# One signal of TensorE per expert tile, down products two tiles behind, and unpaused late scatters

## What is computed

```python
x = x + layernorm(attn(layernorm(x)))    # x: (8, 512, 128) f32, 16 heads of 8, relu MLP 128-512-128 inside
x = x + layernorm(moe(layernorm(x)))
# moe, for each of the 4096 tokens: softmax router over 8 experts, the best 2 are taken
#   g = x @ gate_w[e].T ; u = x @ up_w[e].T       (128 -> 352)
#   y = (silu(g) * u) @ down_w[e].T               (352 -> 128), summed with the two router weights
```

## Time and profile before

| what | value |
|---|---|
| median of 3 runs | 591.68 us (590.68 to 592.72) |
| span of the profiled execution | 596.4 us |
| TensorE busy | 532.1 us, 89% |
| VectorE, ScalarE, GpSimd busy | 63%, 66%, 59% |
| gate and up products, L871 | 111.5 us in 852 passes |
| down products, L881 | 62.5 us in 426 passes |
| indirect DMAs of GpSimd, L1782 and L1793 | 64 and 71, 143.3 us |

### The profile page before, as it was taken

How to read it: one execution, slowest core, us unless ns; L and a number is a source line. 1 busy time by engine, 2 the same in 40 slices (tenths; PEclk the granted TensorE clock), 3 DMA queues, 4 the chain that set the end, 5 groups by cost and what they waited for, 6 DMA issues and landing times.

```text
span 596.4 us, 14609 instructions
## 1 busy us (share of the span) xinstructions
PE 532.1 (89%) x4952; PEld 395.0 (66%) x4969; DVE 375.9 (63%) x1095; ACT 395.4 (66%) x880; POOL 349.7 (59%) x449
## 2 busy tenths in 40 slices
PE   6989899899899899988899899999976899999981
PEld 5655455556566455655555666889976899999960
DVE  6824583965975947996847877527742365555347
ACT  3388989888978788869788696644531355555425
POOL 6104636545538885357877258487578555565545
PEclk9999999999999999999999999999996799999997
DMA  7245333213213322232734512212122203321174
GB/s 196 76 126 161 111 99 109 74 37 108 80 45 122 102 86 71 77 100 78 201 109 134 132 56 52 59 55 69 55 61 69 55 32 86 88 63 32 33 287 141
DMA packets 47016, 55.62 MB, mean 93 GB/s; under 512 B 7376, under 2 KB 41056, under 8 KB 44784
## 3 DMA queue, kind: packets, MB, share of 16 engines
q1 hardware_dynamic: 42624, 45.76, 26.7%
q0 software_dynamic: 4320, 8.92, 4.5%
HBM read 36.27 MB, written 18.92 MB: 93 GB/s over the span
## 4 chain that ended last, share of the span: by engine, by line
PE 56%; DVE 15%; ACT 10%; POOL 6%; issue 6%; DMA 3%; another core or an unknown queue 3%; DVEq 1%; SPq 0%; ACTq 0%; POOLq 0%
PE SC L871 11%; PE OA L748 9%; PE OA L881 6%; PE M L786 4%; PE M L822 4%; PE SC L730 3%; ACT arena L1015 3%; PE SC L734 2%; PE M L643 2%; DVE SS L1330 2%; PE SC L740 2%; PE M L662 1%; POOL slots L1782 1%; PE M L852 1%
## 5 line engine op out<-in xcount | busy, mean ns | idle before, releaser
L1015 ACT ACTIVATE arena<-SC 128x1024 f32<-128x1024 f32 x160 | 161.9, 1039 | 14.7 <-PE SC L735 11.8
L871 PE MATMUL SC<-arena 128*128 128x128 f32 (+1 forms) x852 | 111.5, 283 | 0.0
L871 PEld LDWEIGHTS SC<-arena 128*128 128x128 f32 (+1 forms) x852 | 104.0, 191 | 0.4 <-issue 0.3
L748 PE MATMUL OA<-arena 128*32 128x256 f32 (+1 forms) x1536 | 88.9, 349 | 6.6 <-DVE arena L455 2.8
L1782 POOL DMA_INDIRECT slots<-XBA,IDX x64 | 72.6, 1134 | 37.0 <-DVE IDX L1455 19.6
L1503 DVE TENSOR_TENSOR arena<-arena,SC 128x256 f32<-128x256 f32 (+1 forms) x142 | 43.7, 348 | 68.6 <-issue 24.6
L881 PE MATMUL OA<-arena 128*128 (+1 forms) x426 | 62.5, 284 | 12.9 <-issue 8.1
L748 PEld LDWEIGHTS OA<-arena 128*32 128x32 f32 x1536 | 39.2, 109 | 44.0 <-issue 22.8
L881 PEld LDWEIGHTS OA<-arena 128*128 128x128 f32 (+1 forms) x426 | 55.2, 198 | 15.4 <-issue 15.4
L454 POOL TENSOR_TENSOR arena<-arena 128x512 f32<-128x512 f32 x32 | 42.7, 1335 | 36.2 <-ACT arena L1015 35.6
L447 POOL TENSOR_TENSOR arena<-arena 128x512 f32<-128x512 f32 x23 | 31.2, 1356 | 48.9 <-ACT arena L1015 48.8
(11 more groups left out here) (244 smaller groups left out, 1086.0 us busy)
## 6 DMA issues: line engine op xcount, KB each, us to landing
arena<-parts SPq DMA_DIRECT2D x90, 192.0 KB
parts<-arena SPq DMA_DIRECT2D x16, 384.0 KB
arena<-ytok SPq DMA_DIRECT2D x8, 512.0 KB, 7.3
XGA<-slots SPq DMA_DIRECT2D x39, 65.0 KB
arena<-slots SPq DMA_DIRECT2D x32, 65.0 KB, 1.9
X<-in_L_attn_x SPq DMA_DIRECT2D x4, 512.0 KB, 5.1
out<-X SPq DMA_DIRECT2D x8, 256.0 KB, 2.5
arena<-parts SPq DMA_DIRECT2D x12, 96.0 KB
```

The source lines that it names most:

```text
L748: mm = pe.matmul(OA[32 * j:32 * j + 32, q0:q0 + n], vals[:, t, 32 * h:32 * h + 32], probs(j), start=first, stop=last, skip_group_check=True)
L871: mm = pe.matmul(SC[0:n, r % 2, 512 * m + P * c:512 * m + P * (c + 1)], WSEL[s % 4][:, I * m + i0:I * m + i0 + n], XGT[r % 2], start=True, ...
L1015: act.activation(EB[u], SC[:, n % 2, :], ACT.Exp).then_inc(exp_done, 1)
```

## The change

TensorE gives one signal per tile, `tile_full`, in place of four. `step(s)` is now: gate of tile `s`, transpose of tile `s + 2`, two of the three up products of `s`, the down product of tile `s - 2`, and the last up product of `s`, which signals. ScalarE waits for that one signal and then does its three jobs in the order copy of tile `s + 2`, result of tile `s - 2`, Silu of `s`. TensorE gets waits for the Silu and the product of tile `s - 2` before it writes their banks again (`sg_rdy`, `h_rdy`). From tile 24 on, odd tiles use the two M1 banks for the transpose and for the result. HTB has three buffers. One step more is run at the end (`STILES + 2`).

GpSimd's clearings are gone. The scatters of batch 5 stand one by one at units 2 to 15 of body 8 (`LATE5_AT`), and all 16 of batches 6 and 7 at unit 3 of body 9 (`LATE67_AT`), ahead of that unit's `put`. `put` runs two tiles behind. Batch 7 has a buffer of its own for its rows (XBL, in the space of the exponentials), and its wait for the scatters of batch 5 moves from VectorE to GpSimd.

```diff
-    dict(yroot=6, aroot=9, xroot=13, sc0=3, sc1=4, sc2=4, sc3=5, sc4=5, sc5=6, sc6=7, sc7=8))
+    dict(yroot=6, aroot=9, xroot=13))
+LATE5_AT = (2, 4, 6, 8, 10, 12, 14, 15)
+LATE67_AT = 3
+DOUBLE = 24
...
+        def turned(s):
+            return (M1S[0] if s >= DOUBLE and s % 2 else M0)[:, 0:P]
+        def result(s):
+            return (M1S[1] if s >= DOUBLE and s % 2 else OA)[:, 0:P]
+        def had_bank(s):
+            return s - 1 if s <= DOUBLE else s - 2 if s > DOUBLE + 1 else -1
...
@@ TensorE
+            def xt(s):
+                r, it = s % RING, s // RING
+                pe.wait_ge(xg_in[r], 16 * (it + 1))
+                if had_bank(s) >= 0:
+                    pe.wait_ge(xt_rdy, had_bank(s) + 1)
...
+                return pe.transpose(turned(s), XG[r][:, 0:D], IDN[:, :])
...
+            def down(s):
+                off = weights_offset(pe, s)
+                pe.wait_ge(h_rdy, s + 1)
+                if had_bank(s) >= 0:
+                    pe.wait_ge(ys_rdy, had_bank(s) + 1)
...
-            def step(s, r, it):
-                if s + 1 < STILES:
-                    xt(s + 1, r + 1, 16 * (it + 1 + (r + 1) // RING))
-                if s < STILES:
-                    gu(s, r)
-                if s >= 1:
-                    down(s - 1, r + 1, woff(s - 1))
+            def step(s):
+                if s < STILES:
+                    pe.wait_ge(wsel_rdy, s + 1)
+                    pe.wait_ge(xt_rdy, s + 1)
+                    if s >= 2:
+                        pe.wait_ge(sg_rdy, s - 1)
+                    half(s, 0, range(NIC))
+                    if s + 2 < STILES:
+                        xt(s + 2)
+                    if s >= 2:
+                        pe.wait_ge(h_rdy, s - 1)
+                    mm = half(s, 1, range(NIC - 1))
+                if s >= 2:
+                    mm = down(s - 2)
+                if s < STILES:
+                    mm = half(s, 1, (NIC - 1,))
+                mm.then_inc(tile_full, 1)
...
@@ ScalarE
+            def step(s):
+                act.wait_ge(tile_full, s + 1)
+                if s + 2 < STILES:
+                    evac_x(s + 2)
+                if s >= 2:
+                    evac_y(s - 2)
                 if s < STILES:
-                    silu(s, r)
-                if s >= 1:
-                    evac_y(s - 1, r - 1)
+                    silu(s)
...
@@ VectorE
-            def hidden(s, r):
+            def hidden(s):
                 dve.wait_ge(sg_rdy, s + 1)
-                dve.wait_ge(up_full, s + 1)
...
@@ GpSimd
                 for k in choices:
-                    if b >= NB - 4:
-                        pause()
                     pool.indirect_dma_start(out=slots_d.ap(), ...)
...
             def put(s, r):
-                pause()
                 pool.wait_ge(ys_rdy, s + 1)
...
+                    if b == NB and n in LATE5_AT:
+                        scatter(NB - 3, LATE5_AT.index(n) // 2, (LATE5_AT.index(n) % 2,))
+                    if b == NB + 1 and n == LATE67_AT:
+                        for k in range(2 * T):
+                            scatter(NB - 2 + k // T, k % T)
                     for s in early_tile(b, n):
-                        if s >= 1:
-                            put(s - 1, (s - 1) % RING)
+                        if s >= 2:
+                            put(s - 2, (s - 2) % RING)
```

More of the change, by code:

```diff
@@ L478, in lots_at, with xb @@
             return [i] if 0 <= i < NWT else []
+        def xb(b):
+            return XBL if b == NB - 1 else XB[b % 2]
+        def turned(s):
[4 more added lines that the diff above has]
+            return s - 1 if s <= DOUBLE else s - 2 if s > DOUBLE + 1 else -1
         def early_tile(b, n):
@@ L853, in weights @@
                 mm.then_inc(wt_full, 1)
[L858 to L867, removed]
-                    pe.wait_ge(xt_rdy, s + 1)
[L869 to L873, removed]
@@ L875, in down @@
-            def down(s, r, off):
-                pe.wait_ge(h_rdy, s + 1)
-                if s >= 1:
-                    pe.wait_ge(ys_rdy, s)
-                for c, (i0, n) in enumerate(IC):
-                    mm = pe.matmul(OA[:, 0:P], HTB[r % 2][0:n, P * c:P * (c + 1)],
-                                   WALL[0:n, bass.ds(off + 2 * I + P * c, P)], start=c == 0, stop=c == NIC - 1)
-                mm.then_inc(y_full, 1)
-            def woff(s):
-                return weights_offset(pe, s)
@@ new lines, in half @@
+            def half(s, m, chunks):
+                for c in chunks:
+                    i0, n = IC[c]
+                    mm = pe.matmul(SC[0:n, s % 2, 512 * m + P * c:512 * m + P * (c + 1)], WSEL[s % 4][:, I * m + i0:I * m + i0 + n],
+                                   XGT[s % 2], start=True, stop=True)
+                return mm
+            def down(s):
[3 more added lines that the diff above has]
+                    pe.wait_ge(ys_rdy, had_bank(s) + 1)
+                for c, (i0, n) in enumerate(IC):
+                    mm = pe.matmul(result(s), HTB[s % 3][0:n, P * c:P * (c + 1)],
+                                   WALL[0:n, bass.ds(off + 2 * I + P * c, P)], start=c == 0, stop=c == NIC - 1)
+                return mm
@@ L908, in early @@
                     pe.wait_ge(table_rdy, 2)
[L909 removed]
+                step(s)
             pe.wait_ge(const_rdy, 1)
@@ L995, in _ @@
             pe.wait_ge(table_rdy, 3)
-            for s in range(EARLY, STILES + 1):
-                step(s, s % RING, s // RING)
-            keep_busy(29)
+            for s in range(EARLY, STILES + 2):
+                step(s)
+            keep_busy(29, SC[:, 0, :])
             for b in BY_TENSOR:
@@ L1169, in _ @@
                     if b == NB and n == 0:
-                        evac_x(0, 0)
-                        step(0, 0)
+                        for s in range(2):
+                            act.wait_ge(xt_full, s + 1)
+                            evac_x(s)
+                        step(0)
                     if b == 0 and n in TABLE_AT:
@@ L1217, in _ @@
                         if s > 0:
-                            step(s, s % RING)
-            for s in range(EARLY, STILES + 1):
-                step(s, s % RING)
+                            step(s)
+            for s in range(EARLY, STILES + 2):
+                step(s)
             act.preload_act_table_set("natural_log_exp_and_others")
```

91 lines of the change are left out of this document (47 added, 44 removed).

## The result

The changed kernel took 611.96 us (610.44 to 614.14, 4 runs) beside 592.2 us (590.68 to 595.68, 4 runs) of the kernel before: a ratio of 1.0317, interval 1.0283 to 1.0351. It is 3.2% slower, where the prediction had 1.6% faster.

A forecast was written before the change was run, and what follows sets the result against it. Late TensorE signals beside GpSimd's indirect DMAs were taken to cost 21.0 us; 21.0 - 3.8 - 3.5 - 1.8 - 2.0 - 0.3 = 9.6 us won of 596.4, scaled to 582.2 us; forecast's range 576 to 589, overall 572 to 594.

The forecast's parts named there:

- one signal per DMA is more than enough for one per 2.12 us: Tiles beside GpSimd's DMAs: with a 1.27 us DMA period, one signal a tile suffices; the stretch gives back 21.0 us.
- One TensorE signal gets through per indirect DMA: Bad stretch, tiles 19 to 39: 1.3 us per signal read as matching GpSimd's 1.49 us period, within 15%.
- Rival B: Slower: clearings let signals through, so the unbroken scatter block stops TensorE 18.4 us; 6.8 us slower, 598.4 us; chance 0.16.
- Tile distance: Down product two tiles behind: 0.6 us to spare per tile, taken as 0, bound 6 us.
- Loads: Tiles 31 to 39: loads late behind the scatter block and SyncE's pace, 3.8 us lost, bounds 0 and 10.5.
- Table: Transpose of tile 40: VectorE's table wanted sooner and made later, a stall of 3.5 us.
- Clock: Behind the tile 40 gap: about a tile at half clock level, 1.8 us lost, bounds 0 and 4.
- Units of bodies 8 and 9: TensorE waits at three places, 4.1 us new less 2.1 recovered: 2.0 us lost, bounds 2 won, 6 lost.
- Tail: Last tile's chain: an added copy and later Silu, less a clearing; 0.3 us lost, range -0.4 to 1.

The follow-up runs named there:

- e3: The kernel before without its 103 clearings and nothing else changed; 609.34 us, ratio 1.0244.
- e8: The changed kernel with only the table of the last 31 tiles made 5 tiles sooner; 608.88 us, ratio 1.0193.
- e17: The changed kernel with a probe: VectorE itself waits for TensorE's tile signal, then clears one column; 613.83 us, ratio 1.0301.
- first trace: The profile of the unmodified changed kernel from the first comparison, which measured 611.96 us, ratio 1.0317.
- e14: The changed kernel itself, run again in a session without late signals; 592.29 us, ratio 1.0192.
- e13: The kernel before, unmodified, profiled again in a session without late signals; 580.05 us (one run).
- e2: The changed TensorE, ScalarE and VectorE with GpSimd's old program (103 clearings, scatters at the old units); 602.47 us, ratio 1.0146.
- e5: The changed kernel with clearings ahead of every scatter of batches 4 to 7 and every put; 608.11 us, ratio 1.0170.
- e6: e5 with the table of the last 31 tiles made five tiles sooner; 603.18 us, ratio 1.0112.
- e18: e2 with the table of the last 31 tiles made 5 tiles sooner; 600.38 us, ratio 1.0091.
- e7: e6 with a clearing ahead of only every fourth scatter, puts keeping theirs; 609.36 us, ratio 1.0184.
- e1: The changed kernel with a clearing and its wait ahead of each of the 16 scatters of batches 6 and 7; 607.38 us, ratio 1.0231.
- e4: The changed kernel, no clearings, its 16 scatters one by one at units 3 to 18 of body 9; 606.64 us, ratio 1.0231.

## Why the prediction was wrong, step by step

**The step that failed** is "one signal per DMA is more than enough for one per 2.12 us". It rests on "One TensorE signal gets through per indirect DMA", read from two rates that agreed within 15%. There is no such rate. Beside a run without a clearing a signal waited for up to 12.3 us in the kernel after, and in two of six sessions none waited at all. The reading cannot be mended by another rate: a signal may be taken in the middle of such a run (e3, e8, e17) or only behind its end. For the stretch from tile 19 to 39 the sum had 21.0 - 3.8 - 3.5 - 1.8 = 11.9 us won, and 8.2 us were lost. Against the traces without late signals (44.5 and 53.9 us from tile 19 to 39), late signals cost the kernel before 18.8 us there and the changed kernel 17.6, if nothing else differs between the sessions. One signal in place of four, with the clearings gone, made 1.2 us, less than two runs of one kernel differ.

**Rival B came nearest.** It had TensorE standing for 18.4 us beside the block; the two signals of tiles 20 and 21 waited 6.4 and 12.3 us. Its evidence against, a transpose read at once beside eight scatters, was a single signal and should have weighed less than the two of rows 4, both over 4 us late. B's own time, 598.4, was 13.6 us short of the median. On the scale of the profile it is 596.4 + 6.8 = 603.2, 9.2 us short of the span of 612.4. Of that, to the first transpose +1.8 (the same work, not part of the change); to tile 19 +6.0 where B had 2.0; tiles 19 to 39 71.5 where its terms give 63.3 + 4.5 = 67.8. The other 4.4 us lie in the scale: each run's span is 1.7 to 1.8 us below its time (612.4 and 614.14), so the profiled execution of the kernel before took about 598.2 us, 6.5 above the median of its runs. The prediction carried this over as a ratio. B also asked for a hold from the signal of tile 19 to the end of the block. That signal came at once (its passes end at about 443.0, ScalarE acts at 443.37), and that of tile 20 came in the middle of the block. In the first trace this was just behind the iota, in e8 and e17 ahead of it.

**Tile distance, 0.** Right where no signal is late. Beside the unpaused block in e14 TensorE is busy for 20.80 of 20.80 us.

**Loads, 3.8 us.** 1.6 us in e14 [1.61 before the transpose at 475.07], none in the first trace, where TensorE stood anyway. The block took 22.0 us in e14 (438.24 to 460.28) and 20.1 us in the first trace (441.94 to 462.09); the estimate was 20.8. The difference is VectorE. Timeline of e14:

```profile
453.53 0.96 POOL L1818 DMA_INDIRECT slots<-arena,IDX  x1 [0.30 <-issue]
...
454.69 0.53 DVE L1547 COPY arena<-arena 128x704 f32 x1
454.80 1.25 POOL L1818 DMA_INDIRECT slots<-arena,IDX  x1 [0.30 <-issue]
```

Here an indirect DMA that starts inside a weight copy takes 1.25 us, one beside none 0.96. Seven of the 16 take 1.08 to 1.37 us, each with a weight copy beside it, and the others 0.96 to 1.00. What the seven take over 0.96 us adds up to the 1.9 us. In the block of the first trace, where VectorE mostly had nothing to do, all take 0.96 to 1.00. The rule that the prediction quoted from the Trainium skill, SBUF - State Buffer, "SBUF: two separate sides" (GpSimd cannot write descriptors while VectorE runs such a copy), agrees with these rows, 0.1 to 0.4 us a DMA. The prediction should have priced it at 2 us in place of setting it aside.

The 26.3 ns that the prediction quotes for each signal of TensorE stand in the Trainium skill under another title than the one it names, TensorE: Matmul & The Clock Gate, "The cost: per-tile semaphore tail". No run here shows them, and they entered no term of the sum.

**Table, 3.5 us.** Right: 3.10 and 3.13 us. **Clock, 1.8 us.** Right: behind the gap for the table the granted clock is 0.50 from 487.58 to 490.99 in e14, 3.41 us in which half the passes go, so 1.7 us lost. Windows of e14, columns as in rows 2:

```profile
487.58:490.99 3.41, 3.41 (x18) 3.37 (x17) 0.00 (x0) 0.72 (x4) 0.00 (x0) 0.50 0.29 65
```

**Units of bodies 8 and 9, 2.0 us lost.** 5.3 us without late signals (3.4 to tile 19, 1.9 behind it), near the bound of 6. Of the three places that it named the count shows a longer wait, 1.25 us where it was 0.49. The 2.1 us that were to come back did not, since in a session without late signals there was nothing to give back (63.8 us in e13, 63.4 in the trace of the kernel before), and with them the stage took another 2.2 (69.4 against 67.2). One held signal stands in it, a ScalarE wait of 3.40 us at 419.66, beside five DMAs without a clearing; how much of the 2.2 us is its work is not shown. One place was missed: one gate product waits 0.93 us for VectorE's weight copy, which now stands behind the later product.

**Tail, 0.3 us.** 0.8 us without late signals.

So the costs were sized fairly well (11.4 us foreseen, 13.2 of span measured where nothing is held) and the gain did not exist. In a session without late signals there is nothing to win, and the loss is 2%; in one with them the unbroken runs hold about as much as the paused ones did, and the loss is 3%.

## What to carry to other kernels

Two rates that agree are not a mechanism: before a gain rests on "what is late gets through once per X", find one event in the trace where X happens and the late thing does not follow. Take the kernel before on several sessions first: the medians of its sessions lie between 579.5 and 598.0 us here, and no edit was needed for the difference. Where one signal replaces several, follow each consumer to its next in-order neighbour, for every table, count and copy behind it is later by the same amount, and those terms were the ones that could be foreseen.

## What the runs showed of the hardware

In four sessions of six TensorE's signals came late beside GpSimd's indirect DMAs; in the other two they never did, with the same program (596.4 and 578.3 us of span). Whether that goes with the chip, the core's place on it or the machine is open. The second session (598.0 us) and the fourth (579.5 us) have the same chip number on record, so that number alone does not decide it. Where it occurs, the signal is late for every engine that waits for it (0.04 us apart), those of ScalarE that could be followed beside the same DMAs are not (0.04 us in e17, 0.24 us in the kernel before), and one copy of SyncE was late with it by 1.4 to 1.6 us (first trace, e8, e17). ScalarE's longest wait was 3.9 to 7.0 us with a rest of 0.5 us at each DMA (e2, e5, e6, e18), 10.7 us with one rest in four scatters (e7) and 14.6 to 16.9 us beside ten and more DMAs in a row (first trace, e1, e8, e17). But the length of the run does not settle it: e4, with up to six in a row, had 3.7 us, and e3, with eleven and four signals in a tile, 7.1 us. Where a signal was held past the last DMA of a run of ten and more, it came 2.3 to 3.0 us after that DMA's end (e3 473.76 to 476.06, e1 482.19 to 484.62, first trace 464.62 to 467.63). Why a rest sometimes serves and sometimes not, why some signals come through without one, and whether the signal or the last pass itself is held back, was not settled: a TensorE that waits for its own signal was not tried.
